# Moving four rotation products of the page queries from VectorE to GpSimd

## The reference, cut to what matters

```python
def _rms(x, scale):
    var = jnp.mean(x * x, axis=-1, keepdims=True)
    return x * jax.lax.rsqrt(var + EPS) * (1.0 + scale)

def _rope(x, pos):
    ...
    x1, x2 = (x[..., :half], x[..., half:])
    return jnp.concatenate([x1 * cos - x2 * sin, x2 * cos + x1 * sin], axis=-1)

q = _rope(_rms(q, q_norm_scale), pos)
k = _rope(_rms(k, k_norm_scale), pos)
k_blocks = k_blocks.at[blk, :, off, :].set(k.transpose(0, 2, 1, 3))
...
scores = jnp.einsum('bghtd,bgsd->bghts', qg, k_all) * SCALE
```

## Time and profile before

| | |
|---|---|
| median of 3 runs | 598.15 us |
| lowest, highest run | 594.25 us, 599.76 us |
| span of the profiled execution | 583.4 us |
| own time of the profiled execution | not listed apart from the three runs |
| TensorE, weight load busy | 491.4 us (84%), 372.0 us (64%) |
| VectorE busy | 360.4 us (62%) |
| ScalarE busy | 251.7 us (43%) |
| GpSimd busy | 261.7 us (45%) |
| mean granted TensorE clock | 0.924 of 2.4 GHz |

### The profile page before, as it was taken

How to read it: one execution, slowest core, us unless ns; L and a number is a source line. 1 busy time by engine, 2 the same in 40 slices (tenths; PEclk the granted TensorE clock), 3 DMA queues, 4 the chain that set the end, 5 groups by cost and what they waited for, 6 DMA issues and landing times. The chain is left out here.

```text
span 583.4 us, 10868 instructions
## 1 busy us (share of the span) xinstructions
PE 491.4 (84%) x4205; PEld 372.0 (64%) x4205; DVE 360.4 (62%) x772; ACT 251.7 (43%) x545; POOL 261.7 (45%) x240
## 2 busy tenths in 40 slices
PE   2897799999998999998879899369989893089956
PEld 0586458886886788776653447257767582089956
DVE  3666568886687778854676464958777447034422
ACT  6167754443432444242872334366655241024430
POOL 5045435464353577774650000278870105526650
PEclk9889999999999999998999899859998976579987
DMA  5464763000000122230000008611100001398326
GB/s 171 168 238 141 318 193 90 1 1 1 0 1 1 37 63 64 64 85 35 2 3 1 1 1 321 220 39 27 25 19 2 2 0 62 102 353 284 123 67 206
DMA packets 24724, 51.51 MB, mean 88 GB/s; under 512 B 4265, under 2 KB 16706, under 8 KB 23521
## 3 DMA queue, kind: packets, MB, share of 16 engines
q1 hardware_dynamic: 18704, 40.60, 20.3%
q0 software_dynamic: 5968, 10.22, 5.8%
HBM read 43.97 MB, written 12.37 MB: 97 GB/s over the span
## 5 line engine op out<-in xcount | busy, mean ns | idle before, releaser
L754 PE MATMUL ps<-x_split,gate_up_split 128*128 128x512 f32 x384 | 96.4, 393 | 0.1
L754 PEld LDWEIGHTS ps<-x_split,gate_up_split 128*128 128x128 f32 x384 | 72.0, 188 | 17.2 <-issue 1.5
L2018 POOL DMA_INDIRECT wbig<-new_kv,prepi x40 | 42.9, 1073 | 80.2 <-DMA new_kv<-work 69.0
L947 POOL TENSOR_TENSOR gate_up_split<-wbig,gate_up_split 128x768 fp32r<-128x768 f32 (+1 forms) x24 | 41.6, 1734 | 52.4 <-ACT gate_up_split L887 52.3
L869 DVE TENSOR_TENSOR hidden_split<-work,hidden_split 128x512 fp32r<-128x512 f32 x34 | 37.8, 1110 | 23.1 <-ACT hidden_split L936 23.1
L936 ACT ACTIVATE hidden_split<-work 128x512 fp32r<-128x512 f32 x34 | 21.4, 630 | 59.6 <-DVE work L864 57.5
L778 PE MATMUL ps<-hidden_split,down_split 128*128 128x512 f32 x160 | 42.5, 395 | 2.6 <-issue 1.4
L1959 POOL DMA_INDIRECT chosen<-work,wbig x31 | 30.5, 984 | 28.9 <-issue 15.0
L953 POOL TENSOR_TENSOR down_split<-wbig,down_split 128x384 fp32r<-128x384 f32 (+1 forms) x24 | 29.1, 1213 | 25.9 <-ACT down_split L894 25.8
L2018 POOL DMA_INDIRECT wbig<-in_cache_dram,prepi x32 | 33.5, 1046 | 7.6 <-issue 7.1
L778 PEld LDWEIGHTS ps<-hidden_split,down_split 128*128 128x128 f32 x160 | 29.8, 188 | 10.7 <-issue 4.2
(11 more groups left out here) (326 smaller groups left out, 1174.8 us busy)
## 6 DMA issues: line engine op xcount, KB each, us to landing
work<-in_wE_dram SPq DMA_DIRECT2D x1, 5376.0 KB, 16.3
wbig<-in_wF_dram SPq DMA_DIRECT2D x3, 1664.0 KB, 6.9
sorted<-wmid SPq DMA_DIRECT2D x1, 3999.0 KB, 16.8
wbig<-in_wG_dram SPq DMA_DIRECT2D x1, 3072.0 KB, 10.4
wbig<-in_wE_dram SPq DMA_DIRECT2D x6, 384.0 KB, 3.8
wbig<-chosen SPq DMA_DIRECT2D x8, 256.0 KB, 4.7
wbig<-sorted SPq DMA_DIRECT2D x1, 1935.0 KB, 12.8
wmid<-in_wE_dram SPq DMA_DIRECT2D x5, 384.0 KB, 5.6
```

What stands on the lines that cost most here:

```text
L754: mm = nc.tensor.matmul(o, self.gus[:, w % 2, a, 2 * m + k, :], self.xs[:, b, k, n * HALF:(n + 1) * HALF], start=(k == 0 and a == b), stop ...
L947: nc.gpsimd.tensor_tensor(self.gus[:, k % 2, 1, 0:self.gu_chunks], self.gate_up[:, :, j * P:(j + 1) * P], self.gus[:, k % 2, 0, 0:self.gu_ ...
L2018: return nc.gpsimd.indirect_dma_start(dst, None, table, bass.IndirectOffsetOnAxis(ap=rows.bitcast(U32), axis=0), **({} if bound is None el ...
```

## The change: four products go to GpSimd

For the second half of the queries (`late`, i = 3) `rotate` no longer issues its four products. A new function `rotate_late` issues them on GpSimd, with their outputs in four buffers of their own in `work` (columns 7168 to 8191 and 10240 to 11263). GpSimd runs it after the attention of the stage before and ahead of its wait for the stores of the new keys. The products wait for the raw queries (`page_raw` 4) and the tables, and count on `page_token`. VectorE waits for `page_token` 5 ahead of the difference, in place of its own products; the sum of squares, mean, difference, sum, reciprocal and scaling stay on VectorE.

```diff
+        turns_late = [cut(work, a, 512).rearrange("p (g k f) -> p g k f", g=4, k=8) for a in (7168, 7680, 10240, 10752)]
...
-            dve.wait_ge(sem("page_raw"), i + 1)
-            dve.wait_ge(sem("page_table"), 10 if name == "q" else 6)
-            if n:
-                dve.wait_ge(sem("page_rope"), at - 1)
-            for m, f in enumerate((0, 16, 16, 0)):
-                tt(turns[:, m], raw[:, :, :, f:f + 16], tab[:, m].unsqueeze(2).to_broadcast([P, 4, heads, 16]), ALU.mult)\
-                    .then_inc(sem("page_rope"), 1)
+            late = i == 3
+            if late:
+                at -= 4
+            else:
+                dve.wait_ge(sem("page_raw"), i + 1)
...
+            if late:
+                dve.wait_ge(sem("page_token"), 5)
+            else:
+                dve.wait_ge(sem("page_rope"), at + 4)
+            product = turns_late if late else [turns[:, m] for m in range(4)]
+            tt(o[:, :, :, 0:16], product[0], product[1], ALU.subtract).then_inc(sem("page_rope"), 1)
+            tt(o[:, :, :, 16:32], product[2], product[3], ALU.add).then_inc(sem("page_rope"), 1)
...
+        def rotate_late(pool):
+            heads, raw, _, _, _, _, tab = half_of("q", 1)
+            pool.wait_ge(sem("page_raw"), 4)
+            pool.wait_ge(sem("page_table"), 10)
+            for m, f in enumerate((0, 16, 16, 0)):
+                nc.gpsimd.tensor_tensor(turns_late[m], raw[:, :, :, f:f + 16],
+                                        tab[:, m].unsqueeze(2).to_broadcast([P, 4, heads, 16]), ALU.mult)\
+                    .then_inc(sem("page_token"), 1)
...
             order = [t for q4 in range(B // 4) for t in [B + q4] + list(range(4 * q4, 4 * q4 + 4))]
+            rotate_late(pool)
             pool.wait_ge(sem("page_new"), 32)
```

More of the change, by code:

```diff
@@ L1430, in rotate @@
             at = 7 * i
-            dve.wait_ge(sem("page_raw"), i + 1)
-            dve.wait_ge(sem("page_table"), 10 if name == "q" else 6)
-            if n:
-                dve.wait_ge(sem("page_rope"), at - 1)
-            for m, f in enumerate((0, 16, 16, 0)):
-                tt(turns[:, m], raw[:, :, :, f:f + 16], tab[:, m].unsqueeze(2).to_broadcast([P, 4, heads, 16]), ALU.mult)\
-                    .then_inc(sem("page_rope"), 1)
+            late = i == 3
[3 more added lines that the diff above has]
+                dve.wait_ge(sem("page_raw"), i + 1)
+                dve.wait_ge(sem("page_table"), 10 if name == "q" else 6)
+                if n:
+                    dve.wait_ge(sem("page_rope"), at - 1)
+                for m, f in enumerate((0, 16, 16, 0)):
+                    tt(turns[:, m], raw[:, :, :, f:f + 16], tab[:, m].unsqueeze(2).to_broadcast([P, 4, heads, 16]), ALU.mult)\
+                        .then_inc(sem("page_rope"), 1)
             dve.wait_ge(sem("page_sqr"), i + 1)
```

3 lines of the change are left out of this document (removed).

## The result

The changed kernel took 604.73 us (median of 6 runs, 601.81 to 608.52) beside 598.95 for the kernel before (6 runs, 594.25 to 600.70): a ratio of 1.0123 with an interval of 1.0075 to 1.0171, slower by 1.2%. The forecast was 598.2, in a range of 594.5 to 601.8, and no change. All ratios leave out the runs over 1.5% above the fastest of the same kernel, while the medians are of all runs, so a ratio is not the quotient of two medians.

The account below looks back on a forecast made before the run. VectorE's chain bounds the start of page work, then GpSimd sets the pace; -2.41 and +3.48 made VectorE +1.07 us late, all absorbed, sum 0: 598.2 us, range 594.5 to 601.8.

Parts of the forecast that it names:

- the length of GpSimd's products: Four moved products ahead of the gathers: 1.00 us each, ending at 373.80, 0.16 us before the first gather.
- The wait of VectorE: VectorE's difference of query half 0 waits through all four GpSimd products: +3.48 us, with -2.41 removed making +1.07.
- the pair at 433.49: Two GpSimd products in a row on pages; VectorE's scaling waited through both, taken as evidence for the full wait.
- The feed-forward rows: Rows of the feed-forward stage where VectorE's 1.93 us instruction got in between two GpSimd products, evidence for taking turns.
- Rival 1: VectorE and GpSimd take turns, gathers start +1.2 to +2.1 us late; end +1.5 us (599.7); chance 0.27.
- The gathers' own term: First five gathers on GpSimd meet VectorE products as often as before: 0, within -0.4 and +0.4 us.
- rival 2: Engines don't meet and the gain stays: -1.4 to -2.4 us, 596.5; sign: a 0.68 us difference at 370.2; chance 0.15.
- The limit of 1.65 us to the gain: TensorE's first page work also needs the fifth gather, landing at 383.15, so only 1.65 us could be had.
- The clock rival: Third rival: something else, such as TensorE's clock, moves the end by -3 to +3 us around 598.2; chance 0.08.
- The stated span of the cases: Times of the forecast and its rivals together, said to lie between 595.8 and 600.3 us.
- The pace: GpSimd paces pages from 410 to 435, 7.78 us a round; TensorE and VectorE lateness up to 2.69 us is absorbed.
- The distance around the span: 14.75 us between the profiled span of 583.4 and the median of 598.15, added to the span for the forecast.

Follow-up runs that it names:

- e2: Kernel before with the four products of the second query half left out everywhere, output not the reference's: 600.17 us, ratio 1.0003.
- e16: The edit of e2 again (products left out everywhere) against the kernel before, in another lot: 581.43 us, ratio 0.9956.
- e1_same: The kernel before, unchanged, run as a kernel of its own: 598.44 us, ratio 1.0016.
- short lots: The third and fourth lots of runs, in which the kernel before had medians of 584.49 and 584.37 us.
- e13: The changed kernel once more, in the fourth lot, against the kernel before: 587.83 us, ratio 1.0047.
- e6: Kernel before with two more reductions on VectorE ahead of the scaling of query half 1, GpSimd left alone: 602.71 us, ratio 0.9974.
- long lot: The first or second lot of runs, in which the kernel before had medians of 598.94 and 603.71 us.
- e9: e7 again (stores of the new keys first, experts' weights loaded late) against the kernel before: 584.09 us, ratio 0.9951.
- e14: Kernel before with one added wait: GpSimd's gathers start only after VectorE's difference of query half 1: 587.94 us, ratio 1.0049.
- e10: Changed kernel with SyncE storing the new keys first and loading the experts' weights late, against the kernel before: 587.26 us, ratio 1.0030.
- e4: Kernel before with GpSimd clearing four unused buffers (3072 columns) between its wait and the first gather: 604.04 us, ratio 1.0073.
- e11: Kernel before with stores first, load late, and GpSimd clearing 4096 unused columns ahead of the first gather: 582.01 us, ratio 0.9972.
- e15: Kernel before with stores first, load late, and two of the four products moved to GpSimd: 587.81 us, ratio 1.0051.
- e7: Kernel before with SyncE storing the new keys first, loading experts' weights after GpSimd's sixth product on pages: 597.66 us, ratio 0.9880.

## Why the prediction was wrong

**The failed step is the length of GpSimd's products.** "I take 1.00, since shape, type and engine are the same" measured 1.74 us each, beyond the upper bound of 1.47 as well. The bounds came from rows in which a product met at most one instruction of VectorE. Here four met VectorE in a stretch where it has no gap. 4.05 us became 6.95, the end moved from 373.80 to origin + 17.78, that is 376.81 on the clock of the trace before, and where the products were to end 0.16 us before the gathers begin, the first gather came 3.0 us late. The length and the wait below are one error: by the full wait that was taken for VectorE GpSimd's products would run undisturbed, but in turns each of them waits for VectorE as well.

**The wait of VectorE** was forecast as one of 3.48 us through all four products. It was in turns instead. The extra times in the rows after are 0.91 (1.09 - 0.18), 1.07 (1.75 - 0.68) and 0.69 (1.91 - 1.22), together 2.67, and with -2.41 make +0.26: the spreading started 0.26 late instead of 1.07. The row that decided the choice, the pair at 433.49, was a poor neighbour: VectorE comes to it once with one short instruction. The feed-forward rows, which were put second, were right.

**Rival 1 was the mechanism**, with 0.27 instead of 0.50. It named turns, late gathers and a time of +1.5 us. The Trainium skill ("SBUF — State Buffer", section "Who interferes with whom") gives the shared port pair to whoever issues first for the whole instruction, and counts an instruction of VectorE with two inputs in SBUF among those that contend for it. The rows after agree: the sum, 0.68 us alone, lasts 1.75. Its price was mis-sized: products ending at 375.95 measured 376.81, gathers +1.2 to +2.1 late measured +3.0, and VectorE, 0.45 early by it, was 0.26 late.

**The gathers' own term** held. Between the first and the fifth lie 6.56 us, before 6.69; two of them are lengthened, by 0.60 and 0.74, where three were, by 1.46 in all. "0, within -0.4 and +0.4" was right. The lateness came from ahead of them.

**Rivals 2 and 3.** No gain was kept, since the engines did meet. The sign named for rival 2, a difference of 0.68 us, was there all the same, as it got in between two products: one instruction alone was a poor sign. The limit of 1.65 us to the gain was wrong too: with the products left out (e2, e16) the page work came 2.4 us early, as the gathers got shorter too. The clock rival's bounds of 3 us either way were too narrow for the first measurement, where the clock went from 0.924 in the trace before to 0.901; e1_same, without the change, has 0.914. The stated span of the cases, 595.8 to 600.3, also left out this rival's own 595.2 to 601.2.

**The pace.** That GpSimd sets it from 410 to 435 holds in the short lots: 7.78 us a round in e13, as before. From that the forecast argued that up to 2.69 us of lateness would be absorbed. Nothing here contradicts that for TensorE and VectorE (e6 costs nothing, but in a long lot, where the pace is another), and it was of no use, since it was the pacing engine itself that came late. In the long lots the picture does not hold: in the trace after, TensorE's relapses set the pace, none of the scalings of line 1595 is lengthened any more, and GpSimd idles 22.4 us before its products on pages (20.0 in e1_same).

**The distance around the span.** 14.75 us were added to the span as if they lay outside it. They don't: 1.8 us do. The profiled execution took about 585 us, while the three runs beside it took 594 to 600. The forecast thus argued from an execution of another kind than those it was to predict. All nine profiles of the changed kernel's first measurement and of the long lots have a pause of over 1.4 us of ScalarE or VectorE in the page stage that ends on "remote"; none of the eight of the short lots, nor the trace before, has one. TensorE's waits on its products with the values that end on "issue" go the same way: on line 1527 alone 7 of them in e1_same, 4.1 us in all and the longest 1.2, none in the trace before, e9 and e13. So the pauses come with the lot, and the repeated falls to half clock behind them. In e1_same the page stage is 12 us longer than in the trace before and the rest behind it 4.6.

**What is shown, and what not.** In the short lots the loss of the changed kernel comes from the lateness of the gathers: +3.3 us in the means of e13 (587.60 against 584.31; 2.7 by the ratio), with a chain that is 3.1 us late. e14 reproduces it with a wait alone, and e10 takes the gain of early stores away. By what path it reaches the time is argued: GpSimd's rounds in e13 speak for the pace, but the full clock also came back over 3 us later in e10, e13 and e14, and no run holds the one still and moves the other. e4 gives 0.7% for late gathers only in a long lot, where GpSimd does not set the pace; how the lateness costs there is open. That the change cost 1.2% in its first measurement and 0.5% in two others is not explained: the pauses and the clock vary from run to run, and 6 runs hold few of them. That moving the load by itself brings something is not excluded (e11). And e15 stands against reading the time off the gathers alone: earlier gathers, 0.5% slower, with a clock that came back 13.7 us later.

**Probabilities.** Slower by more than 1% had 0.04, and the range ended at 601.8. Both rested on three runs and one trace; the measured spread of this one kernel between lots, 584 to 604 us, is over five times the largest term of the sum (3.48). The later ratios, 1.0054 and 1.0047, are within 1%. With the 3.0 us of the late gathers added the forecast would have been 601.2, and the measured 604.73 lies 3.5 above that: the failed step accounts for a part of the miss.

**A version that beats both** is stores first with the products left on VectorE (e7 and e9): 0.9880 and 0.9951 of the kernel before, in both lots under 1, though the second is within the scatter of its medians (584.09 against 584.49).

## What to carry to other kernels

An engine that idles in front of a chain of small transfers is not free: count how late its last added instruction ends, at the length that it has beside a busy VectorE (here 1.74 us instead of 1.0), because where that engine sets the pace a delay is carried through the following rounds (3.1 us in e13, of which 1.9 were left at the end of the stage). Ask before moving work what the idle engine is waiting for; here it was a store behind an unrelated load, and moving the load (0.9880 and 0.9951) gained at least as much as leaving the four products out altogether (1.0003 and 0.9956). Before costing an edit, compare the profiled span with the runs: where they are more than a few us apart, the trace is of another kind of execution, and a control run of the same kernel must say which differences belong to the kernel at all. And where the granted clock of the two traces differs in a stretch, write that down as a rival of its own.

## What was not expected of the hardware

- Products of GpSimd and work of VectorE in turns: 1.74 us for a product of 1.00 to 1.05. Also an instruction of VectorE with one small input (L1446, 128x32) is held, 1.09 against 0.18 us.
- A gather that starts in a VectorE instruction with two inputs in SBUF waits for its end and then takes its usual 1.0 us: in e14 the scaling ends at 381.34 + 1.23 = 382.57, and the gather at 381.39 + 2.14 = 383.53; in the trace after the same holds at 374.47 (end 376.21, scaling's end 375.32). The Trainium skill ("SBUF — State Buffer", same section) infers that such a VectorE instruction leaves the writing of descriptors alone. The rows show the gather held all the same. As these gathers also take their row numbers from SBUF (`prepi`), whether it is the reading or the writing that is held is not shown.
- One kernel had medians of 584 us in two lots and of 599 and 604 in two others. The chip that gave 599 is listed under the same number as one that gave 584 later, so the chip alone does not explain it.
- Behind the pieces at 2.4 GHz in which TensorE had been busy for 1.44, 1.47 and 1.90 us, in the trace after, 10.3, 10.2 and 6.8 us at 1.2 GHz followed, though it was then busy without a gap in two of the three (10.20 and 6.80 us). A pause of TensorE thus costs more than itself. What makes the pauses ("remote", "issue") in some lots and not in others stays open.
